# Attention maxima over turned 32x32 blocks, placed by GpSimd and spread by one matmul per bank, with the scores clamped

## The reference, cut to what matters

```python
att = _bn(concat([qk, qr, kr]), gamma_att, beta_att).reshape(...).sum(axis=1)
att = softmax(att, axis=-1)                                   # over i
att_v = einsum('nhpi,nhci->nhcp', att, v * gate_v)
att_vp = einsum('nhpi,cpi->nhcp', att, v_pos * gate_v_pos)
```

## Time and profile before

| | us |
|---|---|
| median of three runs (19908.0 to 19925.6) | 19914.85 |
| the profiled execution: its own time | 19934.48 |
| its span, first to last instruction | 19932.7 |
| attention stage in it | about 2249 to 6663 |
| PE busy in the span | 12303.2 (62%) |
| DVE busy | 10240.1 (51%) |
| ACT busy | 5555.9 (28%) |
| POOL busy | 9274.9 (47%) |
| mean granted TensorE clock | 0.687 |

### The profile page before, as it was taken

The page is one execution under the profiler, slowest core; times in us unless marked ns, Lnnn a source line. Parts: engine busy times, 40 slices in busy tenths (PEclk is TensorE's granted clock), DMA queues, the critical chain, the costliest instruction groups (busy, mean ns, idle before and its releaser), DMA issues. The chain is left out here.

```text
span 19932.7 us, 218211 instructions
## 1 busy us (share of the span) xinstructions
PE 12303.2 (62%) x73490; PEld 6114.6 (31%) x73490; DVE 10240.1 (51%) x14652; ACT 5555.9 (28%) x7765; POOL 9274.9 (47%) x8026
## 2 busy tenths in 40 slices
PE   5553699999999302333333233333347899999999
PEld 2551366666666201111111111111112233333333
DVE  4557544444444343443444344444432577777777
ACT  1114333333333100000000000000000477777776
POOL 0113100000000105886888688678830477777777
PEclk9555555565556555666666665665669999999999
DMA  4104222222222394335333533533333202120211
GB/s 94 31 23 101 58 37 38 37 36 37 38 37 36 114 204 117 96 94 131 94 95 95 130 95 93 130 96 94 96 90 71 44 21 45 22 45 20 44 22 30
DMA packets 1402846, 1408.51 MB, mean 71 GB/s; under 512 B 774780, under 2 KB 1119116, under 8 KB 1386636
## 3 DMA queue, kind: packets, MB, share of 16 engines
q1 hardware_dynamic: 1109964, 742.85, 18.5%
q0 software_dynamic: 221184, 604.27, 10.5%
q10 hardware_dynamic: 70976, 50.83, 0.8%
HBM read 1036.74 MB, written 276.84 MB: 66 GB/s over the span
## 5 line engine op out<-in xcount | busy, mean ns | idle before, releaser
L1359 POOL DMA_INDIRECT dc_g<-corners,dc_idx x4608 | 5299.1, 1150 | 1326.2 <-issue 1246.8
L1975 POOL TENSOR_TENSOR df_sq<-df_sq 128x512 f32<-128x512 f32 x1920 | 2519.3, 1324 | 1951.2 <-ACT df_sq L1923 1906.0
L1432 PE MATMUL dc_ps<-ident,dc_s 128*128 128x128 f32 x2560 | 673.5, 428 | 4348.4 <-DVE dc_s L1523 4345.6
L2070 DVE SCALAR_TENSOR_TENSOR df_pr<-df_pk,vecs,df_h 128x512 f32<-128x512 f32 x2880 | 2094.7, 743 | 613.1 <-PE df_pk L1864 342.1
L1079 POOL TENSOR_TENSOR nz_vp<-nz_vp,nz_den 128x2048 f32<-128x2048 f32 x16 | 105.8, 6611 | 4836.2 <-DMA nz_den<-den_d 4836.2
L1515 DVE TENSOR_TENSOR dc_g<-dc_g,dc_wt 128x2304 f32<-128x2304 f32 x512 | 1309.0, 2557 | 1809.9 <-DMA dc_g<-corners,dc_idx 1809.8
L1923 ACT ACTIVATE df_sq<-df_pk,vecs 128x512 f32<-128x512 f32 x2880 | 1936.7, 685 | 984.7 <-DVE df_pr L2070 961.6
L1432 PEld LDWEIGHTS dc_ps<-ident,dc_s 128*128 128x128 f32 x2560 | 471.4, 218 | 4532.3 <-DVE dc_s L1523 3162.7
L1392 ACT ACTIVATE dc_st<-dc_ps 128x512 f32<-128x512 f32 x640 | 327.0, 607 | 4752.4 <-PE dc_ps L1432 4744.6
L916 DVE TENSOR_REDUCE at_mx<-at_pt 128x4 f32<-128x512 f32 x1024 | 708.4, 692 | 1612.1 <-PE at_pt L779 1612.1
L1861 PE MATMUL df_pk<-df_t,df_wp 64*128 64x512 f32 x3840 | 1348.8, 641 | 218.0 <-ACT df_sq L1923 158.9
(11 more groups left out here) (271 smaller groups left out, 19058.0 us busy)
## 6 DMA issues: line engine op xcount, KB each, us to landing
df_h<-df_h SPq DMA_DIRECT2D x160, 512.0 KB, 7.1
dc_g<-corners,dc_idx POOLq DMA_INDIRECT x4608
corners<-dc_xt SPq DMA_DIRECT2D x16, 4160.0 KB
dc_xp<-x SPq DMA_DIRECT2D x8, 4096.0 KB
cv_xp<-x SPq DMA_DIRECT2D x8, 4096.0 KB, 52.8
y<-sp_p SPq DMA_DIRECT2D x128, 192.0 KB, 2.8
y<-sp_p SPq DMA_DIRECT2D x64, 384.0 KB, 4.3
at_a<-y SPq DMA_DIRECT2D x64, 384.0 KB
```

What stands on the lines that cost most here:

```text
L1359: nc.gpsimd.indirect_dma_start(gt[:, r, k, :, :].rearrange("p a c -> p (a c)"), None, image, bass.IndirectOffsetOnAxis(ap=idx[:, s, r, k:k ...
L1432: i = nc.tensor.transpose(ps[:, j, 128 * r:128 * r + 128], sm[:, r % 2, 128 * j:128 * j + 128], env.ident[:, :])
L1975: nc.gpsimd.tensor_tensor(a, a, sq[:, (KK * n + other) % RING, :], ALU.add).then_inc(nadded, 1)
L2070: nc.vector.scalar_tensor_tensor(out=rows(pr[:, j % RING, :]), in0=rows(pk[:, j % BANKS, :]), scalar=env.vecs[:, bias:bias + 1], in1=shift ...
```

## The change

Per group, DVE now takes the maxima straight from X: `tensor_reduce` with `apply_transpose` turns each 32x32 block and reduces it, which gives for each block of 32 keys the maxima of its 32 queries (`mx` is 128x64 per step: key block and query within its block on the partitions, matrix and query block on the free axis). One f32 matmul turns `mx` (64x128), DVE takes the maximum over the four key blocks from PSUM (`combine`, 64x32), GpSimd multiplies this by a 0/1 pattern into a 64x512 bf16 tile in which each row stands in its own place (`place`), and one matmul per group with a 0/1 matrix spreads it over the partitions of a bank. The transposes of X are gone, and so is ACT's copy of the maxima. After each subtraction DVE takes the minimum of X with 0.25 in an instruction of its own. `subbed` is now counted by that second instruction. The 0/1 patterns are a new input of 64x528 f32, loaded once.

```diff
-        mx = sb("at_mx", [128, 2, 16])
-        mt = sb("at_mt", [16, 2, 128], BF16)
+        mx = sb("at_mx", [128, 2, 64])
+        mt = sb("at_mt", [64, 2, 32])
+        md = sb("at_md", [64, 2, 16, 32], BF16)
...
         @block.gpsimd
         def _(pool):
+            def place(u, e):
+                pool.wait_ge(mt_out, u + 1)
+                nc.gpsimd.tensor_tensor(md[:, e, :, :], mt[:, e, :].rearrange("p (o c) -> p o c", o=1).broadcast_to([64, 16, 32]),
+                                        own[:, :].rearrange("p (r o) -> p r o", o=1).broadcast_to([64, 16, 32]), ALU.mult
+                                        ).then_inc(placed, 1)
...
-            def rows_of_maxima(k, s, q):
+            def transposed_maxima(k, s, q):
                 u = 4 * k + q
                 pe.wait_ge(maxed, 4 * u + 4)
...
+                nc.tensor.matmul(pss[0:64, 0, 0:128], mx[:, q % 2, :], env.ident[:, :], start=True, stop=True).then_inc(mt_done, 1)
             def spread(k, s, q, t):
                 u = 4 * k + q
-                pe.wait_ge(mt_out, u + 1)
...
+                pe.wait_ge(placed, u + 1)
+                if not (isinstance(u, int) and u < 1 and t < 2):
                     pe.wait_ge(subbed, 4 * u + t - 1)
...
+                nc.tensor.matmul(ptt[:, t % 2, :], sel[:, t, :], md[:, q % 2, :, :].rearrange("p r c -> p (r c)"),
+                                 start=True, stop=True).then_inc(mb_done, 1)
...
-            RELS = {1: ((0,), (1,), (2,), (3, 4)), 2: ((5,), (6,), (7,), (8, 9)), 3: ((10,), (11, 12), (13,), (14, 15))}
+            RELS = {1: ((0, 1, 2), (3, 4)), 2: ((5, 6, 7), (8, 9)), 3: ((10, 11, 12), (13, 14, 15))}
...
+                    for t in range(2):
+                        if not (first and q == 0):
+                            spread(*prev, t)
                     qk(k, s, q, (2, 3))
...
+                        for t in range(4):
+                            times_v(*older, t, before)
+                    for part in range(2):
                         if q == 0 and not first:
-                            times_vpos(k - 1, 1 - s, t, lambda: pe.wait_ge(av_out, 4 * k - 1))
+                            for f in (2 * part, 2 * part + 1):
+                                times_vpos(k - 1, 1 - s, f, lambda: pe.wait_ge(av_out, 4 * k - 1))
...
+                        if part == 0:
+                            if q < 3:
+                                qk(k, s, q + 1, (0, 1))
...
+                            transposed_maxima(k, s, q)
...
+                        if t == 0 and not (first and q == 0):
+                            combine(*prev)
...
+                        nc.vector.tensor_reduce(mx[:, q % 2, 16 * t:16 * t + 16], x4(t).rearrange("p (a c) -> p a c", c=32),
+                                                AX.X, ALU.max, apply_transpose=True).then_inc(maxed, 1)
...
+                nc.vector.tensor_reduce(mt[:, q % 2, :], pss[0:64, 0, 0:128].rearrange("p (g c) -> p c g", c=32),
+                                        AX.X, ALU.max, negate=True).then_inc(mt_out, 1)
...
-                    nc.vector.tensor_tensor(x4, ptt[:, t % 2, :], x4, ALU.add).then_inc(subbed, 1)
+                    nc.vector.tensor_tensor(x4, ptt[:, t % 2, :], x4, ALU.add).then_inc(clamped, 1)
+                    dve.wait_ge(clamped, n + 1)
+                    nc.vector.tensor_scalar(x4, x4, 0.25, None, ALU.min).then_inc(subbed, 1)
```

More of the change, by code:

```diff
@@ L626, in _, with attention @@
                                             ).then_inc(low, 1)
[L629 removed]
+def attention(env, posrev, picks, y1, y2, v_dram, av_d, den_d, vp_d):
     nc = env.nc
@@ L675, in _ @@
                          ).then_inc(posl, 16)
+            sp.dma_start(pick[:, :, :].rearrange("p t j -> p (t j)"), picks[:, 0:512]).then_inc(picks_in, 16)
+            sp.dma_start(own[:, :], picks[:, 512:528]).then_inc(picks_in, 16)
             sp.wait_ge(poss, 4)
@@ L733, in _ @@
         def _(pool):
-            nc.gpsimd.tensor_copy(sel[:, :], env.ident[0:16, 0:16]).then_inc(sel_set, 1)
+            def place(u, e):
[3 more added lines that the diff above has]
+                                        ).then_inc(placed, 1)
+            pool.wait_ge(picks_in, 32)
+            nc.gpsimd.tensor_copy(sel[:, :, :], pick[:, :, :]).then_inc(sel_set, 1)
+            for e in range(2):
+                place(e, e)
+            with pool.Fori(0, 2 * NBLK - 1) as v:
+                for e in range(2):
+                    pool.wait_ge(mb_done, 8 * v + 4 * e + 4)
+                    place(2 * v + e + 2, e)
         def stream(eng, work, start, end):
@@ L767, in loads_of @@
                 return (k - s) * (8 * LOADS) + 16 * LOADS
-            def transposed(k, s, q, t):
-                n = 16 * k + 4 * q + t
-                pe.wait_ge(added, n + 1)
-                if t < 2:
-                    if not (isinstance(n, int) and n < 2):
-                        pe.wait_ge(subbed, 16 * k + 4 * q - 4 + t + 3)
-                else:
-                    pe.wait_ge(maxed, n - 1)
-                for e in range(4):
-                    nh = 16 * q + 4 * t + e
-                    last = nc.tensor.transpose(ptt[:, t % 2, 128 * e:128 * e + 128], X[:, s, nh, :], env.ident[:, :])
-                last.then_inc(t_done, 1)
-            def rows_of_maxima(k, s, q):
+            def transposed_maxima(k, s, q):
                 u = 4 * k + q
@@ L848, in work @@
                     qk(k, s, q, (2, 3))
-                    pk, ps_, pq_ = (k, s, q - 1) if q else (k - 1, 1 - s, 3)
-                    ppk, pps, ppq = (k, s, q - 2) if q >= 2 else (k - 1, 1 - s, q + 2)
-                    for t in range(4):
+                    for t in range(2, 4):
                         if not (first and q == 0):
-                            spread(pk, ps_, pq_, t)
-                        if not (first and q < 2):
-                            if q == 1:
-                                before = lambda: pe.wait_ge(vp_out, 4 * (k - 1) + 4)
-                            elif first and q == 2:
-                                before = lambda: None
-                            else:
-                                before = lambda: pe.wait_ge(av_out, 4 * k + q - 2)
-                            times_v(ppk, pps, ppq, t, before)
@@ L863, in work @@
-                    for t in range(4):
-                        transposed(k, s, q, t)
+                            spread(*prev, t)
+                    if not (first and q < 2):
+                        if q == 1:
+                            before = lambda: pe.wait_ge(vp_out, 4 * (k - 1) + 4)
+                        elif first and q == 2:
+                            before = lambda: None
+                        else:
+                            before = lambda: pe.wait_ge(av_out, 4 * k + q - 2)
+                        for t in range(4):
+                            times_v(*older, t, before)
@@ L900, in work @@
                 for q in range(4):
+                    prev = (k, s, q - 1) if q else (k - 1, 1 - s, 3)
+                    x4 = lambda t: X[:, s, 16 * q + 4 * t:16 * q + 4 * t + 4, :].rearrange("p a b -> p (a b)")
                     for t in range(4):
@@ L934, in start, with end @@
                 c.run(nc.vector.tensor_tensor(pb[:, 2, :], pr[:, :], pb[:, 1, :], ALU.subtract))
-            stream(dve, work, start, lambda: subtract(NBLK - 1, 1, 3))
+            def end():
+                combine(NBLK - 1, 1, 3)
+                subtract(NBLK - 1, 1, 3)
+            stream(dve, work, start, end)
         @block.scalar
@@ L943, in rel_to_x @@
                                      ACT.Copy).then_inc(rel_out, 1)
-            def rows_out(k, s, q):
-                u = 4 * k + q
-                act.wait_ge(mt_done, u + 1)
-                if not (isinstance(u, int) and u < 2):
-                    act.wait_ge(mb_done, 4 * u - 4)
-                nc.scalar.activation(mt[:, q % 2, :], pss[0:16, 0, 0:128], ACT.Copy).then_inc(mt_out, 1)
             def exp(k, s, q):
@@ L979, in work @@
                     prev = (k, s, q - 1) if q else (k - 1, 1 - s, 3)
-                    if not (first and q == 0):
-                        rows_out(*prev)
                     if not (first and q < 2):
```

52 lines of the change are left out of this document (22 added, 30 removed).

## The result

The changed kernel takes 20026.59 us (median of five runs, 20004.85 to 20043.48) against 19914.85 (19907.92 to 19928.95): a ratio of 1.0055 [1.0040, 1.0069], 0.4 to 0.7% slower. The forecast was 20310. The profiled execution took 20017.86 us, 83 more than that of before. The attention stage, from its first scores to the last copy of the last block's position groups, is 107 us longer; the rest of the program differs by -24 us between these two executions and was not changed.

What follows compares the result with a forecast made beforehand. TensorE set the pace before; afterwards a chain of waits through the engines would. Steps of 15.8, 19.9, 23.5 and 15.2 sum to 74.4 us a block against 68.0, +403 us over 63 blocks: 20310 us, range 19950 to 20600.

Steps and rivals of the forecast that it cites:

- The waits that were named: Attention stage: spreads wait for DVE's clamp and for POOL; third relative groups wait for ACT's copy behind the exponential.
- the idle end of step 3: TensorE idle about 3 us at each such end, behind the chain copy, addition, combine, place; that step 19.9 against 16.58 us.
- the ring: Each attention step becomes one chain of waits through the engines, spread to next spread; four steps sum to 74.4 us a block.
- the sign of 75 to 80%: Attention stage: PE's busy share falls from 94% to this, while the stage grows to about 4800 us.
- nothing is won: One attention step: the 4 us of transposes are gone, yet it takes 15.8 us against 15.60.
- step 2: One of a block's four attention steps: chain of 15.8 us against 15.60, with 11.3 us of TensorE's own work.
- the low end: DVE's clamp of 512 f32 elements: 0.4 us as lower bound, 0.533 taken, an addition's 0.72 as upper.
- the near end: DVE's turned reductions: 0.69 us each, costing nothing within 5.0 us of room for four; far end 2.38.
- rival 4: Turned reductions at 2.38 us each exceed their room: 605 us on top, 20920 us; 5%.
- Rival 1: Faster: the removed TensorE transposes are all won, 1048 us, giving 18870 us; 4%.
- Rival 3: No change within 0.2%: waits are shorter than forecast, with times_v going on while ACT exponentiates; 5%.
- Rival 2: Faster: TensorE is granted 2.4 GHz in all steps, block 64.3 us, 233 us off, 19680 us; 6%.

Runs made afterwards that it cites:

- clamp_late: Changed kernel with four subtractions first, then four clamps, third and fourth spreads waiting only for the subtraction: 19772.31 us, 0.988 of the changed kernel.
- v_first: Changed kernel with TensorE's times_v matmuls issued ahead of the third and fourth spreads: 19811.31 us, 0.990 of the changed kernel.
- rel_first: Changed kernel with two relative groups ahead of the third spread and their ScalarE copies ahead of the exponentials: 19559.35 us, 0.978 of the changed kernel.
- place_twice: Changed kernel with GpSimd doing the placing product twice, once into an unread buffer: 20176.21 us, 1.009 of the changed kernel.
- idle_turns: Changed kernel with four identity transposes added on TensorE in each step ahead of the third and fourth spreads: 20111.26 us, 1.001 of the changed kernel.
- no_clamp: Changed kernel without the clamp after each subtraction: 19830.28 us, 0.987 of the changed kernel, 0.9926 of the kernel before.
- combine_first: Changed kernel with VectorE's combine ahead of the first addition of a step: 19998.04 us, 0.996 of the changed kernel.
- all_four_long: all_four with four blocks instead of two in the loop's body on TensorE, VectorE and ScalarE: 19172.47 us, 0.959 of the changed kernel.
- all_four: Changed kernel with combine_first, v_first, clamp_late, three relative copies ahead of exponentials, and clamps behind reductions in two steps: 19203.98 us, 0.959 of the changed kernel.

## Why the prediction was right in kind and too large

**Bound and mechanism: right.** The work that was removed had set the pace, and taking it away still brought no time, since the step became a ring through VectorE, ScalarE and GpSimd. The waits that were named are there, the idle end of step 3 is 2.87 us (about 3), and clamp_late, v_first, rel_first and place_twice each moved the time as a link of that ring would, while idle_turns did not, as work off the ring should. TensorE's share of the stage fell to 70%; the sign of 75 to 80% was wrong in itself, since 4129 less the 1048 us removed is 3081, 64% of the 4800 us forecast.

**Direction: right, but only because of the clamp.** Slower was forecast with or without it: with plain subtractions of 0.69 the ring's 74.4 us fall by 2 x 0.56 x 4 = 4.5 to 69.9, still above 68.0 (an estimate from the prediction's own terms). no_clamp has 66.5 against 68.9. So "nothing is won" by taking the transposes away was wrong: 2.4 us a block are won, and the clamp takes 4.0.

**The step that failed: the sum of the ring.** +395 us were forecast and +112 measured, 283 too many. What failed are terms of the sum: the pair of subtraction and clamp and times_v were made too long, and the block before, from which the difference is taken, was made too short. The two errors point the same way and together make 303 us, 20 more than the miss: 8 of these are the rounding of the forecast (403 to 395), 11 lie between the blocks (101 us) and the medians of the runs (112).

1. The ring's terms, 74.4 us a block against 70.5: 3.9 x 63 = 246 us. Step by step it was 19.9, 23.5, 15.2 and 15.8 against 18.87, 22.53, 14.31 and 14.95, so 0.85 to 1.03 us in each step. For step 2:

| link | forecast | measured |
|---|---|---|
| first spread to addition | 1.72 | 1.60 |
| two additions | 1.43 | 1.33 |
| to the fourth spread: two pairs of subtraction and clamp | 2.60 | 2.25 |
| fourth spread, times_v, to ACT's copy | 2.84 | 2.50 |
| copy, exponential, to the third relative group | 3.00 | 2.94 |
| relative group, scores | 1.89 | 1.94 |
| maxima turned, to combine | 0.50 | 0.72 |
| combine to place | 0.40 | 0.37 |
| place to the next spread | 1.38 | 1.30 |
| sum | 15.76 | 14.95 |

The two mis-sized terms are the clamp (0.35 us too long) and times_v (0.34); of the other 0.12 us no term is more than 0.22 off, up or down. That both stand on the chain of every step is shown by no_clamp and v_first, which shorten every step. The clamp was taken from L425 (533 ns, on 64 partitions) with 0.4 as the low end; it lasts 0.427, and the next subtraction starts 0.34 us behind a clamp's start, before its recorded end. A pair comes every 1.06 us and not every 1.25. times_v was taken at the spacing that it has between spreads in the kernel before: three groups at 0.54 and 0.68 from the start of the last one to ScalarE's copy, 2.30 in all. In one piece its 16 matmuls take 1.83 us (4060.74 to 4062.57), and the copy starts 1.96 us behind the first. The prediction also gave, as another sum, the rule of the Trainium skill (TensorE: Matmul & The Clock Gate, Wait — 56ns, not 53.3ns?) for 512 columns, an estimate of 0.43 us a spread. The trace lies between that and the 0.54 of the sum: two spreads and what follows stand 0.96 apart (4055.02 to 4055.98), 0.48 each, and the fourth spread takes 0.54 until times_v begins. The Trainium skill (VectorE: DVE Perf Modes, Mode 2×_2P — use both read ports for one tensor) says that an f32 tensor_scalar from SBUF to SBUF gets two results a cycle, and an f32 tensor_tensor, which needs a port for each of its tensors, one. The trace agrees in direction: 427 ns for the clamp against 683 for the subtraction of the same size, 0.63 of its time and not half of it. By that page the clamp had to come out well under the subtraction's 0.69, so the low end was the one to lean to.

2. The block before, 68.0 us against a mean of 68.9: 0.9 x 63 = 57 us. I read one block out of the timeline. From first scores to first scores, as it was read, the means of steps 2, 3, 0 and 1 are 15.60, 16.50, 22.23 and 14.56 us; the block had 15.60, 16.58, 21.73 and 14.10. So its steps 0 and 1 were short. Step 0 takes two values in turn, 21.6 us in the mean in one block and 22.9 in the next, and the block was one of the first kind. In the other kind TensorE stands still in step 0, just behind the jump of the engines' loop of two blocks, with nothing that it waits for:

```profile
3973.79 0.70 PE L759 MATMUL at_pq<-at_a,at_k 24*128 24x128 bf16 x5 [1.89 <-issue]
```

combine_first and all_four_long put the same alternation at the loop's jump; no run changed the loop of before. In the changed kernel the step hardly alternates (18.86 and 18.93 us for step 3), presumably because its wait for place (2.87 us) covers the stall at the jump; combine_first, which shortens that wait, brings it out.

**Single terms that held.** place 1.04 us for 1.28, within its ends, on the path at the end of step 3 and level with TensorE's own side to 0.13 us at the ends of steps 1 and 2, as the prediction's 15.76 and 15.74 had it. Combine 0.28 for 0.30. The turned reductions: 2.48 us for four, one every 0.62, the near end (0.69); they stay hidden in their 5 us of room, and rival 4 falls. The last spread of step 2 comes 5.18 us behind the first, where 5.7 were given. DVE busy 2446 us in the whole stage, where 2800 were given: the clamps and reductions are each shorter, and the stage too.

**The rivals.** Rival 1 (the removed work is won) is what all_four comes near: its 57.5 us a block, with the clamp, need the order that lets TensorE go on. Rival 3 (no change within 0.2%, since waits are shorter than forecast) is missed as a number, since 0.4 to 0.7% is clear of it. Its reason is the one that came half true: the measured 112 us lie nearer to nothing than to 395. Rival 2 (a higher clock in all steps) did not come; over ten microseconds of a cold step the clock, the third number from the end, is 0.50:

```profile
4060.00:4070.00 10.00, 8.66 (x84) 6.48 (x85) 6.29 (x12) 4.57 (x6) 1.04 (x1) 0.50 0.22 44
```

## What to carry to other kernels

When an engine that was busy for 94% of a stage loses a quarter of its work, follow the new chain through all engines before counting the gain: here 1.0 ms of matmuls left, and the time rose by 0.6% with the clamp and fell by 0.7% without it, until four moves in the lists brought 4%. An instruction costs by its place: a 0.43 us clamp cost 1.3% inside the loop of spread and subtraction and nearly nothing behind it (66.7 us a block in clamp_late, 66.5 in no_clamp). Time an instruction in the surroundings that it will have: times_v between other matmuls took 0.54 us a group, in one piece 0.46. Take the pace of a loop from its mean over many turns, not from one turn.

## What the runs showed of the hardware that I had not expected

- The turned 32x32 reduction of 128x512 f32 comes every 0.62 us, where the ordinary reduction of the same size from PSUM took 692 ns on average in the kernel before.
- In the reordered kernel the step at a loop's jump is longer by 2.3 to 4.9 us with two blocks in the body (all_four) and by 5.3 to 9.4 with four (all_four_long), and the profile names no cause for either.
- The granted clock in the slices ahead of the stage was mostly 9 tenths in the changed kernel's profile (the row below) and 5 in that of before, and this changed nothing: the stage began 7 us later. The mean clock of the page (0.733 against 0.687) therefore says nothing of this change; no_clamp and place_twice had 0.688 and 0.683 and lie on either side of it in time.

```profile
PEclk9999855555556555666666666666669999999999
```
